# Loads of the convolution stage on one DMA queue, and a count of thresholds as the floor in the feed-forward block

## The chip, the cores and the metric

The kernel runs on all 8 cores of one Trainium2 chip, each on its own share of the sequence. The metric is the device time in microseconds of the slowest core. Each core has a matrix engine (TensorE, PE in the profile), a vector engine (VectorE, DVE), an activation engine (ScalarE, ACT), GpSimd (POOL) and SyncE (SP). In this kernel POOL and SP compute nothing: they issue DMA transfers, each from a program of its own that runs strictly in order.

## The reference

For x of shape 2 x 4096 x 2048, one layer of two branches that start from the same normalized input:

```python
xn = layernorm(x)
# branch 1: gated long convolution
q, k, v = xn @ Wq.T + bq, xn @ Wk.T + bk, xn @ Wv.T + bv     # 2048 x 2048 each
q, k = dwconv3(q), dwconv3(k)                                # along the sequence
kv = k * v
y = irfft(rfft(kv, n) * rfft(ssm_kernel, n), n)[..., :L]     # causal, 2048 taps
attn = ((y + kv * D_skip) * q) @ Wo.T + bo
# branch 2: feed-forward
h = xn @ W1.T                                                # 2048 -> 8192
a = gelu(clip(round(h / 0.1), -32768, 32767) * 0.1)
ffn = a @ W2.T
out = x + attn + ffn
```

## The kernel before

Each core owns 1024 rows of the output and gets a slab of 3328 rows, for the history of the convolution. The program is a row of stages with a full stop of all engines between them. `_phase1` normalizes the slab and prepares tables in bf16. `_phase2a` and `_phase2b` make kv and q. `_phase3` is the convolution, `_phase4` the projection with Wo, and `_phase5` the feed-forward block with the final sum. The order within a stage is written out by hand: each engine's instructions are put in a list, with waits on counting semaphores (`Builder.wait`, `Builder.tok`, `Builder.dma`, whose `dma_start` is line 196). The last instruction of a step on TensorE raises `T`, each VectorE instruction `V`, each ScalarE instruction `A`. `tok` (line 205) also makes each VectorE instruction wait for the one before it.

**The convolution (`_phase3`, from line 710).** The 2048 channels are taken in `GR` = 4 groups of 512, and each group in four steps.

1. Forward transform: 34 jobs (17 blocks of 128 frequencies, real and imaginary part), each of 24 matmuls (line 807). VectorE copies each result into `X` (line 823, tiles `p_xr` and `p_xi`). Each job needs a table `tf` of 1 MB, loaded by POOL into one of two buffers. Behind each of these loads POOL issues a load `wc` of a piece of W1 and SP a store of it as bf16 (`w_bf`), until 128 pieces are done.
2. If there is a next group, SP issues 32 DMA transposes that bring its kv into the other `kvg` buffer.
3. Pointwise product: for each of the 17 blocks SP loads the real and the imaginary part of the kernel's transform, `p_kr` and `p_ki` (`Kh`, 128 KB each, two buffers). Before block kc it waits until VectorE is done with block kc-2 (lines 840 to 844). VectorE then does six bf16 operations on 128x512 (lines 851 to 861) in place on `X`.
4. Inverse transform: after the last block, TensorE takes 34 tables `ti` (`p_ti`, 256 KB each, four buffers), each with 8 matmuls (line 881). The tables are loaded by POOL and SP in turn (line 871), each after TensorE is done with the table four back. VectorE then forms `y2tm` (lines 895 to 902).

The lists of POOL and SP simply follow these steps, so what is queued ahead of a load on its engine decides when it is issued.

**The feed-forward block (`_phase5`, from line 979).** First W1: 64 blocks of 128 features by 2 halves of 512 rows, so 128 tiles, each of 16 matmuls (line 1039) into one of two PSUM banks. VectorE turns the tile into rounded and clipped values by seven operations on 128x512 in float32. They all use one set of buffers `ub, iib, fb, cb, mb, zb` (tiles `p_u`, `p_ii`, `p_f`, `p_c`, `p_m`, `p_z`), and ScalarE applies gelu (line 1072) from `zb`. The first operation (line 1053) reads PSUM; it waits for the tile's matmuls and for the gelu of the tile before, and TensorE's tile two later waits for it. The operation at line 1053 forms u = 10 h + 4096.5; the next two convert it to int32 and back; lines 1060 and 1062 take 1 off where the conversion went above u, so that the result is the floor. Then W2: 4 column blocks by 64 feature blocks of 8 matmuls (line 1095), whose weights POOL loads from float32 (`p_w<-w2T`), and the final sum.

Of the kernel before, what the change touches and what calls it, by code (L numbers as in the profile page):

```python
# [10 lines left out]
OP = mybir.AluOpType  # L11
# [698 lines left out]
def _phase3(nc, bld, g, env):  # L710
    rec = Rec()
# [5 lines left out]
    gKV = [bld.dsem(f"p3gKV{i}", "sync") for i in range(2)]  # L717
    TFD = 2
    gTF = [bld.dsem(f"p3gTF{i}", "gpsimd") for i in range(TFD)]
    gKH = [bld.dsem(f"p3gKH{i}", "sync") for i in range(2)]  # L720
    TID = 4
    gTI = [bld.dsem(f"p3gTI{i}", ("gpsimd", "sync")[i % 2]) for i in range(TID)]
    gWC = [bld.dsem(f"p3gWC{i}", "gpsimd") for i in range(2)]
    xWC = [bld.dsem(f"p3xWC{i}", "sync") for i in range(2)]
    gDR = bld.dsem("p3gDR", "gpsimd")
# [1 line left out]
    with ExitStack() as P:  # L727
# [52 lines left out]
        for gg in range(GR):  # L780
# [10 lines left out]
            for kc in range(KC):  # L791
                for ri in range(2):
                    gjob = gg * 2 * KC + job
                    par = gjob % TFD
                    eng = "gpsimd"
# [41 lines left out]
            pw_done = {}  # L837
            for kc in range(KC):
                kp = kc % 2
                if kc >= 2:  # L840
                    bld.wait(rec, "sync", "V", pw_done[kc - 2])
                elif gg >= 1:
                    last_same = KC - 1 - ((KC - 1 - kc) % 2)
                    bld.wait(rec, "sync", "V", pw_prev[last_same])
                for ri in range(2):
                    bld.dma(rec, "sync", gKH[kp],
                            Kh[kp][ri][:, :], env["khat_sp"][ri, kc, gg])
                bld.wait(rec, "vector", gKH[kp], bld.c[gKH[kp]])
                s = slice(kc * GSZ, (kc + 1) * GSZ)
                bld.run(rec, "vector", lambda E, s=s, kp=kp:  # L850
                        E.tensor_mul(tmp[:, :], X[0][:, s], Kh[kp][0][:, :]))
                bld.run(rec, "vector", lambda E, s=s, kp=kp:
                        E.tensor_mul(tmp2[:, :], X[1][:, s], Kh[kp][1][:, :]))
                bld.run(rec, "vector", lambda E, s=s, kp=kp:
                        E.tensor_mul(tmp3[:, :], X[0][:, s], Kh[kp][1][:, :]))
                bld.run(rec, "vector", lambda E, s=s, kp=kp:
                        E.tensor_mul(tmp4[:, :], X[1][:, s], Kh[kp][0][:, :]))
                bld.run(rec, "vector", lambda E, s=s:
                        E.tensor_sub(Z[0][:, s], tmp[:, :], tmp2[:, :]))
                pw_tok = bld.tok(rec, "vector", "V", lambda E, s=s:  # L860
                                 E.tensor_add(Z[1][:, s], tmp3[:, :], tmp4[:, :]))  # L861
                pw_done[kc] = pw_tok
            pw_prev = pw_done
            bld.wait(rec, "tensor", "V", pw_tok)
            first = True
            for kc in range(KC):
                for ri in range(2):
                    idx = kc * 2 + ri
                    gidx = gg * 2 * KC + idx
                    par = gidx % TID  # L870
                    eng = ("gpsimd", "sync")[par % 2]
                    if gidx - TID >= 0:
                        bld.wait(rec, eng, "T", inv_mm[gidx - TID])
                    v = bld.dma(rec, eng, gTI[par], ti[par][:, :],
                                env["tbli_sp"][ri, kc * 128:(kc + 1) * 128, :])
                    bld.wait(rec, "tensor", gTI[par], v)
                    last = (kc == KC - 1) and (ri == 1)

                    def pinvmm(E, tc, par=par, ri=ri, kc=kc, first=first,
                               last=last):  # L880
                        return E.matmul(bank(tc)[:, :GSZ],  # L881
                                        ti[par][:, tc * 128:(tc + 1) * 128],
                                        Z[ri][:, kc * GSZ:(kc + 1) * GSZ],
                                        start=first, stop=last)
                    for tc in range(TCHO - 1):
                        bld.run(rec, "tensor", lambda E, tc=tc, f=pinvmm: f(E, tc))
                    inv_mm[gidx] = bld.tok(
                        rec, "tensor", "T", lambda E, f=pinvmm: f(E, TCHO - 1))
                    first = False
# [89 lines left out]
def _phase5(nc, bld, g, env):  # L979
    rec = Rec()  # L980
# [14 lines left out]
    with ExitStack() as P:  # L995
# [7 lines left out]
        ub = sb("p5_u", (128, TJ), F32)  # L1003
        iib = sb("p5_ii", (128, TJ), mybir.dt.int32)
        mb = sb("p5_m", (128, TJ), F32)
        fb = sb("p5_f", (128, TJ), F32)
        cb = sb("p5_c", (128, TJ), F32)
# [17 lines left out]
        for fc in range(FCH):  # L1025
            par = fc % 2
            if fc >= 2:
                bld.wait(rec, ("gpsimd", "sync")[par % 2], "T", w1_tok[fc - 2])
            v = bld.dma(rec, ("gpsimd", "sync")[par % 2], gW1[par],
                        w1c[par][:, :],  # L1030
                        env["w1_bf"][fc * 128:(fc + 1) * 128, :])
            bld.wait(rec, "tensor", gW1[par], v)
            for tj in range(NTJ):
                bnk = job % 2
                if job >= 2:
                    bld.wait(rec, "tensor", "V", ev_tok[job - 2])

                def p5mm(E, b, par, hc, tj):
                    return E.matmul(  # L1039
                        bank(b)[:, :TJ],  # L1040
                        w1c[par][:, hc * 128:(hc + 1) * 128],
                        xn[:, hc * NOWN + tj * TJ:hc * NOWN + (tj + 1) * TJ],
                        start=(hc == 0), stop=(hc == ECH - 1))
                for hc in range(ECH - 1):
                    bld.run(rec, "tensor", lambda E, b=bnk, par=par, hc=hc, tj=tj:
                            p5mm(E, b, par, hc, tj))
                mt = bld.tok(rec, "tensor", "T", lambda E, b=bnk, par=par, tj=tj:
                             p5mm(E, b, par, ECH - 1, tj))
                bld.wait(rec, "vector", "T", mt)
                if ga is not None:  # L1050
                    bld.wait(rec, "vector", "A", ga)
                ev_tok[job] = bld.tok(rec, "vector", "V", lambda E, b=bnk:
                        E.tensor_scalar(ub[:, :], bank(b)[:, :TJ], 10.0, 4096.5,  # L1053
                                        OP.mult, OP.add))
                bld.run(rec, "vector", lambda E:
                        E.tensor_copy(iib[:, :], ub[:, :]))  # L1056
                bld.run(rec, "vector", lambda E:
                        E.tensor_copy(fb[:, :], iib[:, :]))  # L1058
                bld.run(rec, "vector", lambda E:
                        E.tensor_tensor(cb[:, :], fb[:, :], ub[:, :], OP.is_gt))  # L1060
                bld.run(rec, "vector", lambda E:
                        E.tensor_sub(mb[:, :], fb[:, :], cb[:, :]))  # L1062
                bld.run(rec, "vector", lambda E:
                        E.tensor_scalar(cb[:, :], mb[:, :], 4096.0, -32768.0,  # L1064
                                        OP.subtract, OP.max))
                qv = bld.tok(rec, "vector", "V", lambda E:
                             E.tensor_scalar(zb[:, :], cb[:, :], 32767.0, 0.1,  # L1067
                                             OP.min, OP.mult))
                bld.wait(rec, "scalar", "V", qv)
                ga = bld.tok(rec, "scalar", "A",  # L1070
                             lambda E, fc=fc, tj=tj:
                             E.activation(a[:, fc * NOWN + tj * TJ:  # L1072
                                            fc * NOWN + (tj + 1) * TJ],
                                          zb[:, :], AF.Gelu_apprx_tanh))
                job += 1
            w1_tok[fc] = bld.c["T"]
        bld.wait(rec, "tensor", "A", bld.c["A"])
        ev2, w2_tok, st2 = {}, {}, {}
        for eo in range(EON):
            for fc in range(FCH):  # L1080
                par = fc % 2
# [18 lines left out]
                for tc in range(TCHO - 1):  # L1100
                    bld.run(rec, "tensor", lambda E, tc=tc, f=w2mm: f(E, tc))
                w2_tok[(eo, fc)] = bld.tok(rec, "tensor", "T",
                                           lambda E, f=w2mm: f(E, TCHO - 1))
            mmt = bld.c["T"]
            for tc in range(TCHO):
                par = tc % 2
# [15 lines left out]
                elif eo >= 1:  # L1122
# [7 lines left out]
                    lambda E, par=par, eo=eo:  # L1130
# [23 lines left out]
```

How the kernel before makes its waits and increments, by code:

```python
        def fn(E, out=out, in_=in_, h=h, tr=transpose, slow=slow):  # L195
            E.dma_start(out=out, in_=in_, transpose=tr,
                        allow_slow_non_contiguous=slow).then_inc(h, 16)
# [3 lines left out]
    def wait(self, rec, eng, sem, v):  # L201
        h = self.sems[sem]
        rec.add(eng, lambda E, h=h, v=v: E.wait_ge(h, v))
# [1 line left out]
    def tok(self, rec, eng, sem, mk):  # L205
        prev = self.c[sem]
        self.c[sem] += 1
        v = self.c[sem]
        h = self.sems[sem]
        if prev:
            rec.add(eng, lambda E, h=h, prev=prev: E.wait_ge(h, prev))
        rec.add(eng, lambda E, mk=mk, h=h: mk(E).then_inc(h, 1))
        return v
```

## Time and profile before

| what | us |
|---|---|
| two runs | 5645.95 and 5849.39 |
| their median | 5747.67 |
| the profiled execution, its time | 5644.92 |
| its span, first to last instruction, core 0 | 5643.4 |
| spans of the other seven cores | 5569.3 to 5620.4 |
| TensorE busy (matmuls) | 3500.1 (62%) |
| VectorE busy | 1402.5 (25%) |
| ScalarE busy | 413.6 (7%) |

The profile is of core 0, the slowest. The shares of busy time are means over stages with different limits, so each stage has to be read by itself: by its stretch of time, its waits, and its instructions in order.

### The profile page before, as it was taken

The page shows a single profiled execution, that of the slowest core. Times are in us where ns is not written, and L with a number is a line of the kernel's source. Part 1 is how long each engine was busy: PE and PEld are TensorE (multiplying, and loading weights), DVE is VectorE, ACT ScalarE, POOL GpSimd, SP SyncE. Part 2 cuts the span into 40 slices and gives each one's busy share as a digit, 9 for nine tenths or more (in the row PEclk, how much of TensorE's full clock was granted, in tenths as well). Part 3 has the DMA queues.
Part 4 walks back from the last instruction along what each step waited for, and adds up shares of the span by engine and source line. Part 5 has one row for each costly group of instructions (what it writes and reads, how often), then busy time and mean ns, then how long its engine had stood idle before and what let it go on. Part 6 is the DMA issues. An engine that isn't in the chain of part 4 may idle for free. (4 is left out here: it accounts for less than half of the span.)

```text
span 5643.4 us, 52539 instructions; the slowest of 8 cores (5569.3 to 5643.4 us)
## 1 busy us (share of the span) xinstructions
PE 3500.1 (62%) x18560; PEld 1801.3 (32%) x18560; DVE 1402.5 (25%) x2784; ACT 413.6 (7%) x791; POOL 543.3 (10%) x1008
## 2 busy tenths in 40 slices
PE   3777741999990828378277278506666666464644
PEld 1333311888880413133133133202222222121211
DVE  0111130344441400210311311300377772101011
ACT  0111100222220100000000000001111110000000
POOL 0000010111111001011011011000000001111111
PEclk9889875999995969789689699857899999898988
DMA  9878779111106148558559468341311112333343
GB/s 180 189 180 203 186 207 145 31 31 39 39 24 87 25 117 221 145 150 218 140 152 231 126 167 228 106 79 32 83 49 49 49 49 38 64 46 68 42 70 69
DMA packets 419134, 614.48 MB, mean 109 GB/s; under 512 B 228928, under 2 KB 300608, under 8 KB 389312
## 3 DMA queue, kind: packets, MB, share of 16 engines
q0 software_dynamic: 120352, 384.98, 32.2%
q1 hardware_dynamic: 298528, 226.15, 13.7%
q8 instruction: 156, 2.56, 0.2%
q14 instruction: 98, 0.80, 0.0%
HBM read 578.90 MB, written 138.94 MB: 127 GB/s over the span
## 5 line engine op out<-in xcount | busy, mean ns | idle before, releaser
L807 PE MATMUL ps<-p_kvg,p_tf 128*128 128x512 bf16 x3264 | 766.7, 395 | 336.1 <-DMA p_tf<-tblf_sp 161.9
L1095 PE MATMUL ps<-p_w,p_a 128*128 128x512 bf16 x2048 | 519.4, 402 | 397.7 <-DMA p_w<-w2T 279.0
L360 PE MATMUL ps<-p_ssm,p_tf 128*128 128x512 bf16 x2176 | 541.4, 414 | 241.2 <-ACT p_kb L377 153.9
L1039 PE MATMUL ps<-p_xn,p_w 128*128 128x512 bf16 x2048 | 465.8, 381 | 246.9 <-DVE p_u L1053 216.3
L807 PEld LDWEIGHTS ps<-p_kvg,p_tf 128*128 128x128 bf16 x3264 | 322.5, 101 | 780.4 <-issue 446.6
L533 PE MATMUL ps<-p_xq,p_wk 128*128 128x256 bf16 x3328 | 367.4, 273 | 183.8 <-DMA p_ckb<-ckb 183.7
L1095 PEld LDWEIGHTS ps<-p_w,p_a 128*128 128x128 bf16 x2048 | 193.6, 102 | 723.5 <-issue 558.6
L360 PEld LDWEIGHTS ps<-p_ssm,p_tf 128*128 128x128 bf16 x2176 | 224.8, 105 | 557.2 <-issue 348.7
L533 PEld LDWEIGHTS ps<-p_xq,p_wk 128*128 128x128 bf16 x3328 | 326.4, 98 | 223.1 <-issue 184.5
L533 PE MATMUL ps<-p_xq,p_wv 128*128 128x256 bf16 x3328 | 365.4, 273 | 0.0
L1039 PEld LDWEIGHTS ps<-p_xn,p_w 128*128 128x128 bf16 x2048 | 192.1, 98 | 520.7 <-issue 310.3
L881 PE MATMUL ps<-p_xr,p_ti 128*128 128x512 bf16 x544 | 135.2, 393 | 341.5 <-DVE p_xi L861 341.5
L533 PEld LDWEIGHTS ps<-p_xq,p_wv 128*128 128x128 bf16 x3328 | 325.6, 98 | 37.7
L953 PE MATMUL ps<-p_wo,p_y2fm 128*128 128x512 bf16 x512 | 112.5, 383 | 202.4 <-DMA p_y2fm<-y2tm 202.4
L1125 DVE TENSOR_TENSOR p_t<-ps,p_xr 128x512 f32<-128x512 f32 x32 | 22.1, 691 | 865.6 <-PE ps L1095 802.5
L657 PE MATMUL ps<-p2b_xq,p2b_wq 128*128 128x512 bf16 (+1 forms) x768 | 120.7, 309 | 151.1 <-DMA p2b_xq<-xn_sp 142.1
L196 POOL DMA_DIRECT2D p_w<-w2T x256 | 135.5, 530 | 710.7 <-PE ps L1095 698.6
L1053 DVE TENSOR_SCALAR p_u<-ps 128x512 f32<-128x512 f32 x128 | 88.5, 692 | 456.4 <-PE ps L1039 333.8
L562 DVE TENSOR_SCALAR p_cvt<-p_kcm,p_ck,p_ckb 128x256 bf16<-128x256 bf16 x208 | 72.1, 347 | 483.2 <-ACT p_vcm L550 461.3
L418 DVE BATCH_NORM_STATS2 p_st<-p_x 128x6 f32<-128x512 f32 x104 | 72.2, 694 | 463.5 <-DMA p_x<-x_slab 454.7
L823 DVE CAST p_xr<-ps 128x512 bf16<-128x512 f32 x68 | 47.0, 691 | 559.8 <-PE ps L807 559.8
L881 PEld LDWEIGHTS ps<-p_xr,p_ti 128*128 128x128 bf16 x544 | 54.1, 100 | 410.7 <-issue 350.9
(78 smaller groups left out, 2217.1 us busy)
## 6 DMA issues: line engine op xcount, KB each, us to landing
p_tf<-tblf_sp POOLq DMA_DIRECT2D x136, 1024.0 KB, 7.3
tblf_sp<-p_tf SPq DMA_DIRECT2D x34, 1024.0 KB, 14.2
p_wc<-w_lay POOLq DMA_DIRECT2D x128, 256.0 KB, 7.1
w_bf<-p_wc SPq DMA_DIRECT2D x128, 256.0 KB, 5.8
p_w<-w2T POOLq DMA_DIRECT2D x256, 128.0 KB, 3.3
p_x<-x_slab POOLq DMA_DIRECT2D x26, 1024.0 KB, 10.7
p_tf<-fwd_cos POOLq DMA_DIRECT2D x17, 1024.0 KB, 12.7
p_tf<-fwd_sin POOLq DMA_DIRECT2D x17, 1024.0 KB, 10.2
```

Source lines behind the costliest of these rows:

```text
L196: E.dma_start(out=out, in_=in_, transpose=tr, allow_slow_non_contiguous=slow).then_inc(h, 16)
L360: return E.matmul(bank(b)[:, :GSZ], tf[par][:, sc * 128:(sc + 1) * 128], ssm_sb[:, sc * D + gg * GSZ:sc * D + gg * GSZ + GSZ], start=(sc = ...
L418: E.bn_stats(st6[:, 6 * i:6 * (i + 1)], xb[par][:, BCH * i:BCH * (i + 1)]))
L533: return E.matmul(bank(b)[:, :TT], w[:, hc * D + ec * 128:hc * D + ec * 128 + 128], xq[qpar][:, hc * XSP + qoff:hc * XSP + qoff + TT], sta ...
L562: E.tensor_scalar(cvt[:, :TT], kcm[par][:, base:base + TT], cks[:, ec:ec + 1], ckbs[:, ec:ec + 1], OP.mult, OP.add))
L657: return E.matmul(bank(b)[:, :w], wq[:, hc * D + ec * 128:hc * D + ec * 128 + 128], xq[:, hc * QWT + co:hc * QWT + co + w], start=(hc == 0 ...
L807: return E.matmul(bank(b)[:, :GSZ], tf[par][:, pc * 128:(pc + 1) * 128], kvg[kp3][:, pc * GSZ:(pc + 1) * GSZ], start=(pc == g.PC0), stop=( ...
L881: return E.matmul(bank(tc)[:, :GSZ], ti[par][:, tc * 128:(tc + 1) * 128], Z[ri][:, kc * GSZ:(kc + 1) * GSZ], start=first, stop=last)
L953: return E.matmul(bank(b)[:, :EOSZ], y2fm[:, hc * NOWN + tc * 128:hc * NOWN + tc * 128 + 128], wo[:, hc * D + eo * EOSZ:hc * D + (eo + 1) ...
L1039: return E.matmul(bank(b)[:, :TJ], w1c[par][:, hc * 128:(hc + 1) * 128], xn[:, hc * NOWN + tj * TJ:hc * NOWN + (tj + 1) * TJ], start=(hc = ...
L1053: E.tensor_scalar(ub[:, :], bank(b)[:, :TJ], 10.0, 4096.5, OP.mult, OP.add))
L1095: return E.matmul(bank(tc)[:, :EOSZ], a[:, fc * NOWN + tc * 128: fc * NOWN + tc * 128 + 128], w2c[par][:, :], start=(fc == 0), stop=(fc == ...
```

## The change

In `_phase3` the loads `Kh` and all loads `ti` are issued by POOL; before, `Kh` and every second `ti` were issued by SP. The waits that belong to them move along, and the order in which they stand among each other stays. In `_phase5` the floor is computed in another way: m = u - f, where f is the value converted to an integer and back, then a count of how many of the six levels -2, -1, 0, 1, 2, 3 are at or below m, added to f, and 4099 taken off instead of 4096. Since m is between -1 and 1, the count is 2 or 3 and the result is the same floor.

```diff
-    gKH = [bld.dsem(f"p3gKH{i}", "sync") for i in range(2)]
+    gKH = [bld.dsem(f"p3gKH{i}", "gpsimd") for i in range(2)]
     TID = 4
-    gTI = [bld.dsem(f"p3gTI{i}", ("gpsimd", "sync")[i % 2]) for i in range(TID)]
+    gTI = [bld.dsem(f"p3gTI{i}", "gpsimd") for i in range(TID)]
...
                 if kc >= 2:
-                    bld.wait(rec, "sync", "V", pw_done[kc - 2])
+                    bld.wait(rec, "gpsimd", "V", pw_done[kc - 2])
                 elif gg >= 1:
                     last_same = KC - 1 - ((KC - 1 - kc) % 2)
-                    bld.wait(rec, "sync", "V", pw_prev[last_same])
+                    bld.wait(rec, "gpsimd", "V", pw_prev[last_same])
                 for ri in range(2):
-                    bld.dma(rec, "sync", gKH[kp],
+                    bld.dma(rec, "gpsimd", gKH[kp],
                             Kh[kp][ri][:, :], env["khat_sp"][ri, kc, gg])
...
-                    eng = ("gpsimd", "sync")[par % 2]
+                    eng = "gpsimd"
...
                 bld.run(rec, "vector", lambda E:
-                        E.tensor_tensor(cb[:, :], fb[:, :], ub[:, :], OP.is_gt))
+                        E.tensor_sub(mb[:, :], ub[:, :], fb[:, :]))
                 bld.run(rec, "vector", lambda E:
-                        E.tensor_sub(mb[:, :], fb[:, :], cb[:, :]))
+                        E.tensor_single_scalar(cb[:, :], mb[:, :], -2.0,
+                                               OP.is_ge))
+                for lvl in (-1.0, 0.0, 1.0, 2.0, 3.0):
+                    bld.run(rec, "vector", lambda E, lvl=lvl:
+                            E.scalar_tensor_tensor(cb[:, :], mb[:, :], lvl,
+                                                   cb[:, :], OP.is_ge, OP.add))
                 bld.run(rec, "vector", lambda E:
-                        E.tensor_scalar(cb[:, :], mb[:, :], 4096.0, -32768.0,
+                        E.tensor_add(mb[:, :], fb[:, :], cb[:, :]))
+                bld.run(rec, "vector", lambda E:
+                        E.tensor_scalar(cb[:, :], mb[:, :], 4099.0, -32768.0,
                                         OP.subtract, OP.max))
```

How the instructions stand now at three places. SP at the end of the first group's forward transform, before: the loads of the kernel's transform (`p_kr`, `p_ki`) stand behind the 32 transposes of the next group's kv.

```order
L196 DMA w_bf<-p_wc 128x1024 [waits s_p3gWC0]
L196 DMA_TRANSPOSE p_kvg<-kv_sp 128x512 x32
L196 DMA p_kr<-khat_sp 128x512
L196 DMA p_ki<-khat_sp 128x512
L196 DMA p_kr<-khat_sp 128x512
L196 DMA p_ki<-khat_sp 128x512
L196 DMA p_kr<-khat_sp 128x512 [waits s_V]
```

Now SP goes from the transposes straight on to the stores of the next group's pieces of W1.

POOL at the same place, before: from the last table of the forward transform to its half of the inverse tables, then to the next group.

```order
L196 DMA p_tf<-tblf_sp 128x4096 [waits s_T]
L196 DMA p_wc<-w_lay 128x1024 [waits s_p3xWC0]
L196 DMA p_ti<-tbli_sp 128x1024 x2
L196 DMA p_ti<-tbli_sp 128x1024 [waits s_T] x15
L196 DMA p_tf<-tblf_sp 128x4096 [waits s_T]
```

POOL there after the change, with the 34 loads of the kernel's transform (the first seven of them and the last) ahead of all 34 inverse tables:

```order
L196 DMA p_tf<-tblf_sp 128x4096 [waits s_T]
L196 DMA p_wc<-w_lay 128x1024 [waits s_p3xWC0]
L196 DMA p_kr<-khat_sp 128x512
L196 DMA p_ki<-khat_sp 128x512
L196 DMA p_kr<-khat_sp 128x512
L196 DMA p_ki<-khat_sp 128x512
L196 DMA p_kr<-khat_sp 128x512 [waits s_V]
...
L196 DMA p_ki<-khat_sp 128x512
L196 DMA p_ti<-tbli_sp 128x1024 x4
L196 DMA p_ti<-tbli_sp 128x1024 [waits s_T] x30
L196 DMA p_tf<-tblf_sp 128x4096 [waits s_T]
```

So the `Kh` loads no longer have transposes ahead of them, and the first four inverse tables now stand behind the last `Kh` load.

VectorE in the W1 part, one tile before (s_T: the matmuls, s_A: the gelu of the tile before, s_V: VectorE's own last instruction):

```order
L1053 TENSOR_SCALAR p_u<-ps 128x512 [waits s_T,s_A,s_V]
L1056 CAST p_ii<-p_u 128x512 [waits s_V]
L1058 CAST p_f<-p_ii 128x512 [waits s_V]
L1060 TENSOR_TENSOR p_c<-p_f,p_u 128x512 [waits s_V]
L1062 TENSOR_TENSOR p_m<-p_f,p_c 128x512 [waits s_V]
L1064 TENSOR_SCALAR p_c<-p_m 128x512 [waits s_V]
L1067 TENSOR_SCALAR p_z<-p_c 128x512 [waits s_V]
```

And one tile after the change (the numbers of the lines shift):

```order
L1053 TENSOR_SCALAR p_u<-ps 128x512 [waits s_T,s_A,s_V]
L1056 CAST p_ii<-p_u 128x512 [waits s_V]
L1058 CAST p_f<-p_ii 128x512 [waits s_V]
L1060 TENSOR_TENSOR p_m<-p_u,p_f 128x512 [waits s_V]
L1062 TENSOR_SCALAR p_c<-p_m 128x512 [waits s_V]
L1066 SCALAR_TENSOR_TENSOR p_c<-p_m,p_c 128x512 [waits s_V] x5
L1069 TENSOR_TENSOR p_m<-p_f,p_c 128x512 [waits s_V]
L1071 TENSOR_SCALAR p_c<-p_m 128x512 [waits s_V]
L1074 TENSOR_SCALAR p_z<-p_c 128x512 [waits s_V]
```

Thirteen instructions stand where there were seven, in one chain.

## Rows read from the trace of the kernel before

**Rows 1.** Whole run, who waited for whom: us in total, times, longest.

```profile
PE ps L881 <- DVE p_xi L861: 341.5, 4, 95.9
PE ps L1039 <- DVE p_u L1053: 216.3, 124, 2.0
DVE p_tmp L851 <- DMA p_ki<-khat_sp: 120.4, 4, 40.9
```

**Rows 2.** Timeline, end of the first forward transform: start, us, engine, line, operation, [idle before].

```profile
2309.05 41.56 SPq L196 DMA_TRANSPOSE p_kvg<-kv_sp  x32
...
2314.04 0.69 DVE L823 CAST p_xi<-ps 128x512 bf16<-128x512 f32 x1 [8.50 <-PE ps L807]
...
2351.27 0.43 SPq L196 DMA_DIRECT2D p_ki<-khat_sp  x1
...
2353.56 0.42 DVE L851 TENSOR_TENSOR p_tmp<-p_xr,p_kr 128x512 bf16<-128x512 bf16 x1 [38.84 <-DMA p_ki<-khat_sp]
...
2356.74 0.42 DVE L851 TENSOR_TENSOR p_tmp<-p_xr,p_kr 128x512 bf16<-128x512 bf16 x1
```

**Rows 3.** Timeline, the first pointwise operation of the second, third and fourth group.

```profile
2772.38 0.43 DVE L851 TENSOR_TENSOR p_tmp<-p_xr,p_kr 128x512 bf16<-128x512 bf16 x1 [40.87 <-DMA p_ki<-khat_sp]
...
3185.06 0.42 DVE L851 TENSOR_TENSOR p_tmp<-p_xr,p_kr 128x512 bf16<-128x512 bf16 x1 [40.50 <-DMA p_ki<-khat_sp]
...
3546.73 0.42 DVE L851 TENSOR_TENSOR p_tmp<-p_xr,p_kr 128x512 bf16<-128x512 bf16 x1
```

**Rows 4.** Timeline, first group's inverse transform: TensorE's tables and a load by POOL.

```profile
2428.33 1.89 PE L881 MATMUL ps<-p_xr,p_ti 128*128 128x512 bf16 x8
...
2430.06 1.89 PE L881 MATMUL ps<-p_xi,p_ti 128*128 128x512 bf16 x8
2430.76 0.54 POOL L196 DMA_DIRECT2D p_ti<-tbli_sp  x1 [2.92 <-PE ps L881]
```

**Rows 5.** DMA issues, 2410 to 2470, then 2355 to 2405: count, KB, median us to landing.

```profile
p_ti<-tbli_sp POOLq DMA_DIRECT2D x15, 256.0 KB, 2.9
p_ti<-tbli_sp SPq DMA_DIRECT2D x15, 256.0 KB, 3.0
...
p_ki<-khat_sp SPq DMA_DIRECT2D x15, 128.0 KB, 2.2
```

**Rows 6.** DMA issues of the whole run, the pieces of W1.

```profile
p_wc<-w_lay POOLq DMA_DIRECT2D x128, 256.0 KB, 7.1
```

**Rows 7.** Stretches of core 0 (transposes, forward transform, W1): busy by engine, PEclk, DMA share, GB/s.

```profile
2309.00:2352.00 43.00, 4.86 (x17) 1.76 (x15) 0.69 (x1) 0.00 (x0) 0.00 (x0) 0.58 0.46 105
...
2493.00:2727.00 234.00, 187.61 (x795) 78.79 (x793) 22.81 (x33) 0.00 (x0) 35.04 (x66) 0.94 0.82 217
4003.00:4700.00 697.00, 465.84 (x2048) 192.08 (x2048) 484.21 (x896) 81.18 (x128) 17.75 (x33) 0.99 0.15 49
```

**Rows 8.** Timeline, one tile of the W1 part and the start of the next.

```profile
4400.60 0.69 DVE L1053 TENSOR_SCALAR p_u<-ps 128x512 f32<-128x512 f32 x1 [0.95 <-ACT p_a L1072]
...
4401.44 3.61 PE L1039 MATMUL ps<-p_xn,p_w 128*128 128x512 bf16 x16 [1.75 <-DVE p_u L1053]
...
4405.16 0.63 ACT L1072 ACTIVATE p_a<-p_z 128x512 bf16<-128x512 f32 x1 [4.73 <-DVE p_z L1067]
4405.97 0.69 DVE L1053 TENSOR_SCALAR p_u<-ps 128x512 f32<-128x512 f32 x1 [0.95 <-ACT p_a L1072]
```

**Rows 9.** Groups of VectorE instructions, whole run: busy us, mean ns | idle before.

```profile
L566 DVE SCALAR_TENSOR_TENSOR p_cvt<-p_kcm,p_ck,p_cvt 128x256 bf16<-128x256 bf16 x208 | 100.7, 484 | 22.4 <-DVE p_cvt L562 0.9
...
L1060 DVE TENSOR_TENSOR p_c<-p_f,p_u 128x512 f32<-128x512 f32 x128 | 88.6, 693 | 13.3
...
L1064 DVE TENSOR_SCALAR p_c<-p_m 128x512 f32<-128x512 f32 x128 | 54.6, 427 | 13.6
...
L689 DVE SCALAR_TENSOR_TENSOR p2b_cvt<-p2b_qpre,p2b_cq,p2b_cvt 128x512 f32<-128x512 bf16 x32 | 24.0, 751 | 3.3
```

## Prediction

> **What bounds the kernel now.** I read first the table of waits, for the two stages that the diff touches, then the timeline at the place of each wait, then the stretches by engine, and last the groups of instructions for durations.
>
> In the convolution TensorE stands still four times for the pointwise product, 341.5 us in all [rows 1]. It cannot start the inverse transform before VectorE has done all 17 blocks. VectorE itself waits for its first block's load: 120.4 us over four groups, 40.9 at most [rows 1]. The timeline tells why. VectorE is done with the forward transform at 2314.04 + 0.69 us, but SP is busy with 32 transposes from 2309.05 for 41.56 us, and issues the first block's `p_ki` only at 2351.27 [rows 2]. In the second and third group the same wait is 40.87 and 40.50 us. In the fourth, which has no next group to fetch, there is none [rows 3]. Nothing else is late there, so this wait is on the path.
>
> In the W1 part of the feed-forward block one tile takes 4405.97 - 4400.60 = 5.37 us [rows 8]. That is VectorE's chain and nothing else: 692 + 2 x 427 + 2 x 693 + 2 x 427 = 3786 ns of operations, 6 gaps of 13.3 / 128 = 0.104 us between them, and 0.95 us in which VectorE waits for the gelu of the tile that it has just finished [rows 8, 9]. The sum is 5.36 us. (The 692 is line 1053's 0.69 us; the two at 693 have the form of line 1060, the four at 427 that of line 1064.) TensorE does its 16 matmuls in 3.61 us, and before them waits 1.75 us for line 1053 [rows 8], 124 times and 216.3 us in all [rows 1]. So there VectorE has no slack, and each microsecond put on its chain is paid 128 times.
>
> **The change part by part.**
>
> *The queue of the `Kh` loads.* On POOL the first two blocks' loads stand right behind the last forward table, with no wait that is still open. They are issued while TensorE still works on the last jobs, and VectorE can go on 0.1 us after its last copy. What goes is 38.84 + 40.87 + 40.50 = 120.2 us [rows 2, 3].
>
> What is late next? A block takes VectorE 2356.74 - 2353.56 = 3.18 us [rows 2]. With two buffers, the loads for block kc are issued when block kc-2 is done, and hide if they take less than 3.18 us from there. On SP they do. On POOL two things are to be added. The reaction: in the inverse transform the matmuls that POOL waits for end at 2428.33 + 1.89 us, and it issues at 2430.76, 0.54 us later [rows 4]. And POOL spends 0.54 us on each issue [rows 4]. For landing the queues are equal, 2.9 against 3.0 us for the same 256 KB [rows 5], so I take 2.1 for `p_ki` where SP had 2.2. The first load's timeline (issued 2351.27, 2.2 us to land, used 2353.56) leaves 0.09 us for VectorE's start [rows 2, 5]. The sum is 0.54 + 0.54 + 2.1 + 0.09 = 3.27 us. With two buffers a block then takes the mean of 3.27 and 3.18, so 0.05 us more than now.
>
> For some 41.56 / 3.2 = 13 blocks of three groups the transposes now run beside the loads. They take 0.46 of the DMA engines [rows 7]. No row shows a load from POOL beside transposes. The lower bound is no slowing. The upper is a POOL load while the engines are 0.82 busy, as `p_wc` in the forward transform: 7.1 us to land [rows 6, 7], a delay of 0.54 + 0.54 + 7.1 + 0.09 = 8.27 us, and (8.27 + 3.18) / 2 = 5.72 us a block. A share of 0.46 is nearer to the free case. I take 0.5 us more to land, 0.25 us a block: 3 x 13 x 0.30 = 12 us, and 29 other blocks x 0.05 = 1 us. The term is -120 + 13 = -107 us.
>
> The Trainium skill has a rule that speaks against this part. "SBUF — State Buffer", section "Who interferes with whom", says that descriptors for a DMA issued from GpSimd are written by GpSimd itself, and that it is locked out while VectorE runs an operation in a two-port mode. By the same section `tensor_tensor` has no such mode, so the six operations of a block should leave POOL alone; by the trap as it is first told, the loads would starve, as in the second rival below. The trace has no POOL issue beside the six operations.
>
> *The queue of the `ti` loads.* All 34 are now POOL's, behind the last `Kh` load, which is issued 0.54 us after block 14 ends. Six issues of 0.54 us and 2.9 us to land make 0.54 + 3.24 + 2.9 = 6.7 us for the fourth table. TensorE starts when block 16 ends, 6.4 us after block 14, and comes to the fourth table three tables later. In the steady state a table lasts 1.73 us (2430.06 - 2428.33), four buffers leave 3 x 1.73 = 5.2 us, and a load needs 0.54 + 0.54 + 2.9 = 4.0 us at most [rows 4, 5]. So it costs nothing; the cover is 1.2 us, and if it were gone by 1 us, each load would pay a fourth of it, 34 x 4 x 0.25 = 34 us. POOL gets to the next group's `tf` one table later, 1.7 us, with the 17 us of `y2tm` work ahead. The transposes lose nothing: SP issues them when it did, and they have the pointwise product and the inverse transform to land in. The stores of W1 behind them no longer wait on SP for `ti`, but they wait for their own loads anyway. All this is 0.
>
> *The floor.* Per tile two `tensor_tensor` in float32 go (693 ns each) and two come. Added are one `tensor_single_scalar`, taken as the 427 ns of `TENSOR_SCALAR` in float32, and five `scalar_tensor_tensor`. Their nearest row is line 689: 751 ns for 128x512 with one bf16 and one float32 input. From 256 to 512 elements the form goes from 484 to 751 ns [rows 9], 1.04 ns an element and a fixed 217. Six more instructions bring six more gaps. The sum is 0.427 + 5 x 0.751 + 6 x 0.104 = 4.81 us a tile, and 128 x 4.81 = 615 us. Bounds: the row below is `tensor_tensor` at 693 (5 x 0.058 x 128 = 37 us less); the form at half its rate, since now both inputs are float32, is 217 + 2 x 534 = 1285 ns (342 us more); and 693 instead of 427 for the comparison is 34 us more. I take 751, as a float32 `tensor_tensor` with two such inputs shows nothing of a half rate (693 ns, with 534 for 512 elements by the slope above).
>
> The Trainium skill warns of that half rate: "Vector Engine (DVE) Microarchitecture Reference", section "Points that are easy to get wrong", says that the form with two SBUF sources that are not bf16 halves its throughput. No run so far shows it. By that rule the time is the first rival's; by line 689 it is the forecast.
>
> TensorE in this part: its 3.61 us of matmuls per 10.2 us of tile make it idle more, and in the stretch in which it stands almost idle its granted clock is 0.58, near the level of 1.2 GHz, instead of 0.99, that of 2.4 GHz [rows 7]. Even at 1.2 GHz a tile is twice 3.61, 7.2 us, under 10.2. So nothing hangs on the clock. The weight loads come every 20 us instead of every 10.7 and stay hidden. The W2 part is as before.
>
> **The sum.** 5644.9 (the profiled execution: 5643.4 of span and 1.5 around it) - 107 + 615 = 6153 us. The other run of before was 204 us slower, and the median shown, 5747.67, lies halfway; I forecast for executions like the profiled one.
>
> **The rivals.**
>
> *The half rate of the five new operations* (by the rule above): 6153 + 342 = 6495 us. For it: both inputs are float32 in SBUF, as in no row. Against it: `tensor_tensor` reads two such inputs at the full rate [rows 9].
>
> *The loads from POOL are the pointwise product's bound.* If they take 8.27 us throughout, all 15 blocks per group that have to wait cost 2.54 us: 4 x 15 x 2.54 = 152 us against the 13 counted, 6153 + 139 = 6292 us. For it: no margin is left (3.27 against 3.18), and VectorE and POOL work closely together there. Against it: the 2.9 us of POOL's `ti` loads.
>
> *The change does not bring the loads forward*: something else on POOL keeps them until SP's transposes are through. 6153 + 107 = 6260 us. Against it: the order shows nothing open ahead of them.
>
> *Not slower: the added operations lie beside other work.* If the W1 part were bound by TensorE, VectorE's chain could grow free, and only -107 would stay: 5538 us. This decides at 107 / 128 = 0.84 us a tile: what the six operations put on the path must be under 0.14 us each, and the cheapest row of such an operation is 0.427 + 0.104. It would need the wait of 1.75 us before each tile's matmuls to be due to something other than line 1053.
>
> **How the numbers follow.** The forecast gets 0.82, the half rate 0.07, loads from POOL as the bound 0.05, loads not brought forward 0.03, not slower 0.02 and what I don't see 0.01. The range reaches from 6080 (`tensor_tensor`'s 693 ns, no slowing by transposes, and 20 us for the spread among cores) to 6300, which takes in the two rivals on the loads and the 34 us for the comparison; the half rate stays outside. Faster by over 2% (about what a measurement of this kernel can tell from no change) 0.02, within it 0.01, slower 0.97.
>
> **What would show it.** Right: no wait of some 40 us at line 851; blocks of 3.2 to 3.5 us; three waits of TensorE for line 861 near 60 us instead of 95; a tile of the W1 part of 10.2 us, with 751 ns for each of the five operations and TensorE waiting some 6.5 us per tile for line 1053. Wrong: 1285 ns in those operations, blocks over 4 us with a wait for `p_ki` at each, or a tile clearly off 10.2 us.

## The result and the profile after

| | before | after |
|---|---|---|
| median of all runs, us | 5685.11 (10 runs) | 6134.93 (11 runs) |
| profiled execution, us | 5644.92 | 6131.05 |
| its span, slowest core, us | 5643.4 (core 0) | 6129.5 (core 4) |

The changed kernel is slower, by a ratio of 1.0837 with a 95% interval of 1.0794 to 1.0881. The forecast was 6153 us in a range of 6080 to 6300. (In some executions one die runs at a lower clock; the ratios leave these out.)

First the table of waits, whole run, of the changed kernel: who waited for whom, us in total, times, longest. It answers to [rows 1].

```profile
PE ps L1039 <- DVE p_u L1053: 489.8, 120, 5.3
...
PE ps L881 <- DVE p_xi L861: 257.7, 4, 67.7
...
DVE p_tmp L851 <- DMA p_ki<-khat_sp: 40.1, 40, 3.0
```

In the convolution TensorE waits 84 us less for the pointwise product. VectorE's waits for `p_ki` have changed in kind: before 120.4 us in 4 waits, now 40.1 us in 40. The three long waits, one in each group that has a next one, have gone, and short ones, at about every second block, have come.

The timeline of the changed kernel at the first group's pointwise product shows both; it answers to [rows 2].

```profile
2301.39 0.54 POOL L196 DMA_DIRECT2D p_kr<-khat_sp  x1
2301.92 0.54 POOL L196 DMA_DIRECT2D p_ki<-khat_sp  x1
...
2310.76 0.69 DVE L823 CAST p_xi<-ps 128x512 bf16<-128x512 f32 x1 [4.81 <-PE ps L807]
2311.56 0.43 DVE L851 TENSOR_TENSOR p_tmp<-p_xr,p_kr 128x512 bf16<-128x512 bf16 x1
...
2314.21 0.43 DVE L861 TENSOR_TENSOR p_xi<-p_tmp 128x512 bf16<-128x512 bf16 x1
2314.74 0.42 DVE L851 TENSOR_TENSOR p_tmp<-p_xr,p_kr 128x512 bf16<-128x512 bf16 x1
2315.17 0.54 POOL L196 DMA_DIRECT2D p_kr<-khat_sp  x1 [11.64 <-DVE p_tmp L851]
2315.26 0.42 DVE L853 TENSOR_TENSOR p_tmp<-p_xi,p_ki 128x512 bf16<-128x512 bf16 x1
2315.70 0.54 POOL L196 DMA_DIRECT2D p_ki<-khat_sp  x1
...
2319.07 0.43 DVE L851 TENSOR_TENSOR p_tmp<-p_xr,p_kr 128x512 bf16<-128x512 bf16 x1 [1.26 <-DMA p_ki<-khat_sp]
```

The first block's loads are out 9 us before VectorE needs them, and it goes on 0.11 us after its last copy. The third block's loads may be issued when line 861 of the first ends, at 2314.64. POOL reacts 0.53 us later, issues the two in 1.07 us, and the data are used at 2319.07, 4.43 us after the release. By then VectorE has been done with the second block for 1.26 us, since a block lasts 3.18.

DMA issues of the changed kernel, first in that stretch (2309 to 2352 us, beside the transposes), then in the fourth group's (3452 to 3505 us, without them): KB each, median us to landing.

```profile
p_ki<-khat_sp POOLq DMA_DIRECT2D x10, 128.0 KB, 3.1
...
p_ki<-khat_sp POOLq DMA_DIRECT2D x15, 128.0 KB, 2.4
```

So a `p_ki` load through POOL lands in 2.4 us when alone and in 3.1 beside the first group's transposes. Beside those of the second and the third group (2692 to 2731 and 3075 to 3114 us) it takes over a microsecond more:

```profile
p_ki<-khat_sp POOLq DMA_DIRECT2D x9, 128.0 KB, 4.2
...
p_ki<-khat_sp POOLq DMA_DIRECT2D x9, 128.0 KB, 4.3
```

In the W1 part, one tile of the changed kernel (timeline), against [rows 8]:

```profile
4404.70 0.69 DVE L1053 TENSOR_SCALAR p_u<-ps 128x512 f32<-128x512 f32 x1 [0.95 <-ACT p_a L1079]
...
4405.54 5.30 PE L1039 MATMUL ps<-p_xn,p_w 128*128 128x512 bf16 x16 [4.70 <-DVE p_u L1053]
...
4407.36 0.43 DVE L1062 TENSOR_SCALAR p_c<-p_m 128x512 f32<-128x512 f32 x1
...
4407.89 3.88 DVE L1066 SCALAR_TENSOR_TENSOR p_c<-p_m,p_c 128x512 f32<-128x512 f32 x5
4411.87 0.69 DVE L1069 TENSOR_TENSOR p_m<-p_f,p_c 128x512 f32<-128x512 f32 x1
...
4413.77 0.63 ACT L1079 ACTIVATE p_a<-p_z 128x512 bf16<-128x512 f32 x1 [9.25 <-DVE p_z L1074]
4414.58 0.69 DVE L1053 TENSOR_SCALAR p_u<-ps 128x512 f32<-128x512 f32 x1 [0.95 <-ACT p_a L1079]
```

A tile takes 4414.58 - 4404.70 = 9.88 us instead of 5.37. The five new operations last 3.88 us together, the gaps between them included. TensorE's wait has grown from 1.75 to 4.70 us and its matmuls from 3.61 to 5.30. The group of the new instructions, and then the stretches of the W1 and the W2 part (columns as in rows 9 and 7), say the same of the whole:

```profile
L1066 DVE SCALAR_TENSOR_TENSOR p_c<-p_m,p_c 128x512 f32<-128x512 f32 x640 | 443.0, 692 | 66.5
```

```profile
3928.00:5196.00 1268.00, 728.22 (x1994) 254.83 (x2033) 982.50 (x1664) 81.43 (x129) 17.77 (x33) 0.69 0.08 26
5196.00:6129.00 933.00, 523.80 (x2007) 195.87 (x2048) 66.43 (x96) 0.37 (x1) 169.10 (x318) 0.88 0.35 59
```

The new operations take 692 ns each. TensorE's granted clock in the W1 part is 0.69, where it was 0.99. Part of that belongs to this core: cores 4 and 5 had 0.70 over 3928 to 5170 us, the other six 0.73 or 0.74. On core 0, with 0.74, TensorE waits longer for line 1053, and the part is as long (first starts to last starts 3913.0 to 5170.4 us there, 3928.8 to 5186.7 on core 4):

```profile
3928.00:5170.00 1242.00, 706.64 (x1994) 247.22 (x1992) 963.41 (x1633) 79.02 (x126) 17.31 (x32) 0.74 0.08 26
```

```profile
PE ps L1039 <- DVE p_u L1053: 527.3, 125, 5.3
```

Where the time went, from the first and the last start of line 1053 (`p_u`) in both traces, first before (core 0), then after (core 4):

```profile
L1053 DVE TENSOR_SCALAR p_u<-ps x128: 690/692/692, 4013.0 to 4695.7; 128x512 f32<-128x512 f32 x128
```

```profile
L1053 DVE TENSOR_SCALAR p_u<-ps x128: 690/692/693, 3928.8 to 5186.7; 128x512 f32<-128x512 f32 x128
```

All that comes before the W1 part is 4013.0 - 3928.8 = 84 us shorter. The W1 part went from 682.7 to 1257.9 us, 575 more. The rest, up to the end of the span, went from 947.7 to 942.8, 5 less. The sum is +486, the difference of the two spans.

These are two different cores, so the small terms are worth less than they look. On all eight cores the W1 part took 682.6 to 682.9 us before and takes 1257.3 to 1258.1 now. What comes before it is 60 to 100 us shorter on the same core (medians of the cores 4001.1 and 3919.8, 81 less), and TensorE's waits for line 861 are 88 to 98 us shorter. The rest has medians of 922.0 and 922.6. That the 84 us are also what the waits of these two cores lost is a coincidence.

### The profile page after: what moved, and what is told of

Its sections match the earlier page's. It is cut to its first block and busy times, and to the rows that moved or that the text cites. A ratio compares the mean times of both kernels' runs of the same rounds, so it can differ in the third digit from the quotient of the medians.

```text
span 6129.5 us, 53837 instructions; the slowest of 8 cores (6069.5 to 6129.5 us)
## 1 busy us (share of the span) xinstructions
PE 3758.2 (61%) x18322; PEld 1866.9 (30%) x18560; DVE 1900.9 (31%) x3552; ACT 414.2 (7%) x791; POOL 653.9 (11%) x1212
## 5 line engine op out<-in xcount | busy, mean ns | idle before, releaser
L1039 PE MATMUL ps<-p_xn,p_w 128*128 128x512 bf16 x2007 | 733.9, 542 | 551.0 <-DVE p_u L1053 489.8
L1039 PEld LDWEIGHTS ps<-p_xn,p_w 128*128 128x128 bf16 x2048 | 256.8, 130 | 1028.1 <-issue 996.7
L1066 DVE SCALAR_TENSOR_TENSOR p_c<-p_m,p_c 128x512 f32<-128x512 f32 x640 | 443.0, 692 | 66.5
L881 PE MATMUL ps<-p_xr,p_ti 128*128 128x512 bf16 x533 | 133.6, 392 | 258.6 <-DVE p_xi L861 257.7
```

The costliest lines, as they stand in the source:

```text
L881: return E.matmul(bank(tc)[:, :GSZ], ti[par][:, tc * 128:(tc + 1) * 128], Z[ri][:, kc * GSZ:(kc + 1) * GSZ], start=first, stop=last)
L1039: return E.matmul(bank(b)[:, :TJ], w1c[par][:, hc * 128:(hc + 1) * 128], xn[:, hc * NOWN + tj * TJ:hc * NOWN + (tj + 1) * TJ], start=(hc = ...
L1066: E.scalar_tensor_tensor(cb[:, :], mb[:, :], lvl, cb[:, :], OP.is_ge, OP.add))
```

## The experiments

The change has two parts that do not meet. The theory was that they simply add up: less wait for the order of SP's list, more operations on VectorE's chain. Its rival was that one part hides or gives back some of the other. Where a ratio to the kernel before is given, its 95% interval stands with it; the other kernels are read by their profile alone. "Medians of the dies" are the medians of the spans of cores 0 to 3 and of cores 4 to 7.

**1. The loads alone.** The edit is the first half of the diff: `Kh` and `ti` on POOL, the floor as before.

> Only the change in the convolution: all Kh and ti loads on POOL, the floor as before. Theory (the two parts add up; the loads' part is worth the 84 us that TensorE's waits for line 861 lost in the profile after): 84 us less than before, ratio 0.985, the waits for line 861 some 258 us in all. Rival (part of the gain is given back in the next forward transform or in the feed-forward block, hidden in the whole change by the long W1 part): the same waits, but less than 40 us off the time. The prediction's own 107 us would be a ratio of 0.981.

Measured: ratio 0.979, interval 0.9711 to 0.9869. TensorE's waits for line 861 were 253.7 us, 88 less than before, and the medians of the dies were 91 and 87 us shorter (5517.9 against 5609.1, 5514.6 against 5601.9). Nothing was given back; the theory holds. The ratio's interval excludes the rival's 40 us, but does not tell 84 us from 107.

**2. The floor alone.** The edit is the second half of the diff, with the loads as before. It was run twice.

> Only the new floor, the loads as before. Theory: six more operations on VectorE's chain, five of 692 ns: 128 x 4.51 = 577 us more than before, ratio 1.102, a tile of 9.87 us. Rival (the lower granted clock of TensorE in this part also costs something, there or in the W2 part): more than 590 us, with a W2 part longer than before's 942 us.

> The floor-only kernel again, since the runs of the first time were mostly disturbed. Theory: 128 x 4.51 = 577 us more than before, ratio 1.102. Rival (a cost of TensorE's lower clock outside the W1 part): over 1.11 on cores of an undisturbed die.

Measured the first time: the profiled execution took 6273.53 us; there was no ratio. Its cores 0 to 3 took 6174.5 to 6208.7 us, while core 4 had a clock of 0.806 and a W2 part of 993 us. That looked like the rival. But the W2 part was long only on cores 4 and 5 (993 and 984 us), whose granted clock over 5279 to 6270 us was 0.77 and 0.79; on the other six, at 0.89 or 0.90, it took 898 to 938 us. The second time: ratio 1.1064, interval 1.1003 to 1.1125, the W1 part from 4019.9 to 5276.9 us, 574 more than before, and a W2 part of 5286.9 to 6203.9, 917 us. The ratio's interval reaches past the rival's 1.11. The medians of the dies do not: they were 571 and 587 us longer than before, ratios of 1.102 and 1.105, for the 577 us of the theory. So the rival falls: the W2 part need not be longer with the new floor, and the 993 us went with a lower clock that came in one execution and not in the other. The two halves add up: -0.021 and +0.106 are +0.085, and the whole is +0.084.

**3. What makes the blocks late: one more buffer.** On top of the first experiment:

```diff
-    gKH = [bld.dsem(f"p3gKH{i}", "gpsimd") for i in range(2)]
+    gKH = [bld.dsem(f"p3gKH{i}", "gpsimd") for i in range(3)]
...
-              for i in range(2)]
+              for i in range(3)]
...
-                kp = kc % 2
-                if kc >= 2:
-                    bld.wait(rec, "gpsimd", "V", pw_done[kc - 2])
+                kp = kc % 3
+                if kc >= 3:
+                    bld.wait(rec, "gpsimd", "V", pw_done[kc - 3])
```

(The wait for the group before counts by three in the same way.)

> The loads-only kernel with three buffers for Kh instead of two, so that a load is issued when block kc-3 is done and has 6.35 us. Theory (the blocks beside the transposes are late by the latency of one load through POOL, about 4.1 to 5 us against 3.18): VectorE's 40 us of waits for p_ki go to under 5 us, blocks last 3.18 us, and the time is some 36 us under the loads-only kernel. Rival (the transposes leave too little DMA bandwidth, or POOL's issuing is held up by VectorE): the waits stay above 20 us.

Measured: ratio 0.9769, interval 0.9697 to 0.9842. On the profiled core the waits for `p_ki` are gone altogether (up to 3.1 us are left on the others), and TensorE's are at 221.5 us:

```profile
PE ps L881 <- DVE p_xi L861: 221.5, 4, 55.8
```

That is some 55 us a group, for 17 blocks of 3.18 us. The transposes and VectorE still work beside the loads, and `p_ki` still takes 3.6 us to land beside the first group's, so neither the bandwidth nor POOL's issuing was short; only the time from release to use was too long for two buffers. The medians of the dies are 18 and 27 us under the first experiment, for 32 us of waits; by the ratio alone the two can't be told apart.

**4. Which share is POOL's: `Kh` on ScalarE's queue.** On the kernel before:

```diff
-                    bld.wait(rec, "sync", "V", pw_done[kc - 2])
+                    bld.wait(rec, "scalar", "V", pw_done[kc - 2])
...
-                    bld.dma(rec, "sync", gKH[kp],
+                    bld.dma(rec, "scalar", gKH[kp],
```

(The other wait and the semaphores move along.)

> The kernel before with the Kh loads alone on ScalarE's queue, which is idle there; ti as before. Theory (POOL's reaction of 0.54 us and its 0.54 us an issue make the loads late, and beside transposes landing takes longer on top): blocks of 3.2 to 3.6 us beside the transposes, waits for p_ki under 20 us, and some 100 to 115 us less than before. Rival (the transposes alone make the loads late, whatever the queue): waits for p_ki of 35 us or more, as in the profile after, and some 85 us less than before.

Measured: ratio 0.984, interval 0.9759 to 0.992, so 45 to 136 us less, which holds the numbers of both. TensorE waits 239.6 us for line 861, 102 less than before, and VectorE 20.4 us for `p_ki` (18.4 to 28.5 over the cores):

```profile
DVE p_tmp L851 <- DMA p_ki<-khat_sp: 20.4, 23, 2.1
```

The waits are near those of the theory, but the medians of the dies are 84 and 88 us under before, which is the rival's number and not 100 to 115. So ScalarE's queue shortens the waits, and that it is faster than POOL's (91 and 87 us) is not shown. Both theories had a share in the lateness. To tell them apart, here are the mean distances of line 851's starts in the second group, over the 12 blocks beside the transposes and over the last 4, each from the timeline:

| kernel | queue of `Kh` | first 12, us | last 4, us |
|---|---|---|---|
| before | SP, after the transposes | 3.17 | 3.17 |
| loads alone | POOL | 3.83 | 3.39 |
| `Kh` on ScalarE | ScalarE | 3.64 | 3.18 |
| three buffers | POOL | 3.17 | 3.17 |

The other two groups with transposes differ by some tenths: their first 12 blocks took 4.06 and 3.91 us with the loads alone, 3.76 and 3.64 through ScalarE.

Away from the transposes the blocks through ScalarE's queue are not late, and those through POOL are, by 0.2 us. Beside them the blocks through ScalarE are late too. The DMA issues of this kernel in the first group, beside the transposes, show why:

```profile
p_ki<-khat_sp ACTq DMA_DIRECT2D x9, 128.0 KB, 3.8
```

In its fourth group the same load takes 2.2 us. So the transposes lengthen the landing whatever the queue, and POOL adds its reaction and its issues.

**5. The order of SP's list alone.** On the kernel before: the block of transposes is moved behind the loop of the pointwise product, and all `ti` go to POOL so that none stands behind the transposes.

> The kernel before with Kh still on SP, but the transposes behind all Kh loads in SP's list (all ti on POOL, so that none stands behind the transposes). Theory (the 40 us waits were the order of SP's list and nothing else; and the blocks were late only beside transposes and through POOL): no wait for p_ki at all, blocks of 3.18 us, TensorE's four waits for line 861 some 221 us as with three buffers, and the forward transform of the next group not late. Rival (the transposes come too late for the next group, or collide with the inverse tables): the same short waits, but new waits of TensorE for p_kvg or p_ti that give back over 30 us.

Measured: 5534.9 us for the profiled execution, and medians of the dies 94 and 102 us under before. Of the waits for `p_ki` 2.6 us are left (1.7 to 8.8 over the cores), the waits of TensorE for the pointwise product are 223.7 us, and no wait for `p_kvg` came up besides the first group's.

```profile
DVE p_tmp L841 <- DMA p_ki<-khat_sp: 2.6, 5, 0.9
```

(Line 841 is the 851 of the others.) The inverse transform waits a little for its tables beside the transposes:

```profile
PE ps L881 <- DMA p_ti<-tbli_sp: 14.4, 15, 3.0
```

It was 5.7 us before. The theory holds in the main: the 40 us were the order of SP's list, and a queue of its own is not needed for that. The time gained is less than the 118 us of waits; 9 of the difference are these waits for `p_ti`, and the rest stays open.

**6. Constant or pointer.** On the floor-only kernel: three of the five levels come from a 128x1 tile.

```diff
-                for lvl in (-1.0, 0.0, 1.0, 2.0, 3.0):
+                for lvl in (-1.0, 0.0):
...
+                for li in range(3):
+                    bld.run(rec, "vector", lambda E, li=li:
+                            E.scalar_tensor_tensor(cb[:, :], mb[:, :],
+                                                   lv[:, li:li + 1],
+                                                   cb[:, :], OP.is_ge, OP.add))
```

> The floor-only kernel, with three of the five levels (1, 2, 3) read from a 128x1 tile instead of given as constants. Theory (the 751 ns of line 689 came from its scalar per partition, the 692 ns of the new operations from their constants): the three last 751 ns, the other two 692 ns, and the W1 part 128 x 3 x 0.059 = 23 us more than the floor-only kernel. Rival (751 came from the bf16 input): all five last 692 ns.

Measured, groups of VectorE instructions of this kernel:

```profile
L1074 DVE SCALAR_TENSOR_TENSOR p_c<-p_m,p_lv,p_c 128x512 f32<-128x512 f32 x384 | 288.6, 752 | 42.6
...
L1070 DVE SCALAR_TENSOR_TENSOR p_c<-p_m,p_c 128x512 f32<-128x512 f32 x256 | 177.3, 692 | 28.5
```

With everything else equal the scalar from a tile costs 60 ns. The W1 part went from 4017.1 to 5300.2 us, 26 us more than without it. So the row I had taken for the price, line 689, was dearer for its scalar and not for its input types.

**7. Three operations less.** On the floor-only kernel, levels -2, -1 and 0 only.

> The floor-only kernel with only the levels -2, -1 and 0: the floor is the same, since m never reaches 1. Theory (each operation on the chain is paid in full, 0.692 + 0.104 us): a tile of 9.87 - 3 x 0.796 = 7.48 us, 128 x 2.39 = 306 us less than the floor-only kernel. Rival (part of the chain lies beside the matmuls of a TensorE at the lower clock, 6.8 us a tile): less than 250 us off, with TensorE's waits for line 1053 near 0.

Measured: line 1053 starts from 4019.7 to 4973.0 us, so a tile of 953.3 / 127 = 7.51 us, and 304 us less than the floor-only kernel's W1 part. TensorE still waits 331.5 us for line 1053, so the rival falls. Each operation on the chain is paid in full.

**8. gelu off the chain.** On the floor-only kernel, two buffers for the input of gelu in turn, and line 1053 waits for the gelu of two tiles before.

> The floor-only kernel with two buffers for the input of gelu, so that line 1053 waits for the gelu of the tile before the last. Theory (the tile is VectorE's operations and gaps plus the 0.95 us of gelu): a tile of 9.87 - 0.95 + 0.10 = 9.02 us, 108 us less than the floor-only kernel, and VectorE without idle time above the gaps. Rival (TensorE or the loads set part of the tile): less than 60 us off.

Measured: line 1055 (that is the 1053 of the others) starts from 4041.0 to 5197.5 us, a tile of 9.11 us, and the part is 101 us shorter. VectorE's waits for ScalarE are gone; what is left above 9.02 are scattered gaps of 0.5 us in place of 0.1. The tile is the sum of VectorE's chain, this time with VectorE as its only member.

**9. A version that beats both.** `Kh` on POOL with three buffers, and a shorter floor: adding and taking off 1.5 x 2^23 in float32 rounds as the reference does.

```diff
-                        E.tensor_scalar(ub[:, :], bank(b)[:, :TJ], 10.0, 4096.5,
+                        E.tensor_scalar(ub[:, :], bank(b)[:, :TJ], 10.0, 12582912.0,
                                         OP.mult, OP.add))
...
+                        E.tensor_scalar(cb[:, :], ub[:, :], 12582912.0, -32768.0,
+                                        OP.subtract, OP.max))
```

(It takes the place of the conversions, the comparison and the two operations behind it.)

> Both findings used: Kh on POOL with three buffers, and the rounding by adding and taking off 1.5 x 2^23 in float32, which leaves three operations a tile (692 + 427 + 427 ns). Theory (the tile is VectorE's chain until that is shorter than TensorE's matmuls): chain 1.55 + 0.21 + 0.95 = 2.70 us, under TensorE's 16 matmuls of 3.45 us, so TensorE is the bound with about 3.5 us a tile: 128 x 1.87 = 239 us less in the W1 part, with the 120 us of the loads 5645 - 359 = 5286 us, ratio 0.936; no wait of TensorE for line 1053. Rival (TensorE keeps waiting for the bank or a weight load, now that a block of W1 is used up in 7 us): a tile over 4 us and a ratio above 0.95.

Measured: 5258.69 us median, ratio 0.9329, interval 0.9302 to 0.9355, against 0.936 expected; TensorE has no wait for line 1053. The waits and the stretch of the W1 part of this kernel:

```profile
DVE p_u L1053 <- PE ps L1039: 553.1, 127, 340.1
```

```profile
3879.00:4320.00 441.00, 436.18 (x1990) 198.53 (x2029) 197.87 (x384) 81.72 (x129) 17.52 (x33) 1.00 0.22 75
```

Line 1053 starts from 3879.0 to 4317.6 us, a tile of 3.45 us. The wait has turned round: now VectorE waits for TensorE (213 us in 126 waits; the longest, 340.1 us, lies before the first tile), and TensorE is busy 436 of 441 us at a clock of 1.00.

## Why the prediction was right

*The bound of the W1 part.* Right. The chain 4.81 us longer per tile was the main term, and it measured 575.2 / 127 = 4.53 us. The size was off by one duration, in the term 5 x 0.751: five operations at 751 ns were counted and took 692, 5 x 0.059 = 0.30 us a tile and 38 us in all. The lower bound named for them was the right value. I had chosen line 689 because it has the same operation; the sixth experiment shows that its extra 60 ns belong to its scalar from a tile. The forecast's bound from `tensor_tensor`, with the operands alike, was the better neighbour.

*The half rate*, the first rival, is refuted: 692 ns with both inputs in float32, the same as a `tensor_tensor`. It would have been 1285. The warning in the Trainium skill ("Vector Engine (DVE) Microarchitecture Reference", section "Points that are easy to get wrong") does not hold for this operation and shape.

*The wait behind the transposes.* Right: with three buffers TensorE's waits are 341.5 - 221.5 = 120 us shorter, as counted, and the experiment with SP's order (and `ti` on POOL) takes away 118 us without another queue for `Kh`.

*The lateness of loads through POOL.* The mechanism was right, the size too small: 13 us were counted, and VectorE's waits for `p_ki` were 40.1, of which 257.7 - 221.5 = 36 us were on the path. The reaction (0.53) and the issues (1.07 for two) came out as read. What was wrong are the two steps on landing. "I take 2.1 for `p_ki`" was 2.4 us alone, which makes the delay 3.57 us and the block 3.38; the fourth group's took 3.39. "I take 0.5 us more to land" beside the transposes, 2.6 in all, was 3.2, 4.2 and 4.3 us in the three groups (windows as above, the first over 2311 to 2350 us). By the forecast's own sum these make blocks of 3.78, 4.28 and 4.33 us, where it had 3.48, and the first 12 blocks of the three groups took 3.80, 4.13 and 4.17. So the loads' term was -84 between the two profiled cores (-81 by the medians before the W1 part) and not -107.

*POOL held up by VectorE* was not seen: each `p_kr` issue of the changed kernel took 537 to 544 ns, beside the six operations or not. That agrees with what the Trainium skill says of `tensor_tensor` in "SBUF — State Buffer", section "Who interferes with whom", that it has no two-port mode. (It also says that with both inputs in SBUF such an operation contends with GpSimd's reads; these issues show nothing of that.) In the W1 part POOL's loads do fall on operations that take 427 ns where those with two inputs take 692. There an issue is sometimes longer, as this one of the kernel before (timeline):

```profile
4016.83 0.72 POOL L196 DMA_DIRECT2D p_w<-w_bf  x1 [35.64 <-PE ps L1039]
4017.00 0.43 DVE L1067 TENSOR_SCALAR p_z<-p_c 128x512 f32<-128x512 f32 x1
```

It took 0.72 us instead of 0.53. In the changed kernel three of the 31 issues of that part, all beside line 1071, took 0.58, 0.58 and 0.69 us, and the others 0.53; on the other cores the longest took 0.76. Whether those operations run in such a mode no row says; if they do, it cost an issue 0.23 us at most in this part.

*The inverse tables.* Right: behind the last `Kh` load they cost nothing. In the profile of the changed kernel TensorE had no wait for `p_ti`, where before it had 5.7 us.

*TensorE's clock.* Right that nothing hangs on it. The granted clock fell to 0.69, between the levels of 1.2 and 2.4 GHz, the matmuls of the tile shown took 5.30 us instead of 3.61, and TensorE still waited 4.70. The wait was put at 6.5 us by the old 3.61; the sum of both is what the chain fixes. Cores 0 and 4 show it: 0.74 and 0.70 of clock, 527.3 and 489.8 us of waits, and 1257.4 and 1257.9 us for the part. With the chain shortened in the ninth experiment TensorE had no such pauses and had 1.00.

The two misses have opposite signs: the cost of the floor was put 40 us too high (615 for 575) and the gain of the loads 23 us too high (107 for 84). With the 5 us that the rest got shorter on these two cores the total was off by only 22 us, 6153 against 6131 for the profiled execution. That is closer than either term was, so the nearness of the total is luck; that both mechanisms were met is not.

## What to carry to other kernels

A stage whose period is one engine's chain of dependent operations pays for every added operation in full, its gap too, times the number of tiles; read the period from two starts of the same line, check that the chain adds up to it, and price a new operation by a row with the same kinds of operands, its scalar included. A DMA list is strictly in order, so a load that is needed first belongs ahead of a batch that is needed later; changing the order did as much here as another queue. With two buffers compare the time from release to use (reaction, issues, landing beside what then runs) with the period: where they are within some tenths of a microsecond, a third buffer takes nearly the whole wait away (here for 256 KB more of buffers).

## What was not expected of the hardware

- A `scalar_tensor_tensor` of 128x512 in float32 takes 692 ns with a constant and 752 ns with a scalar read from a 128x1 tile.
- POOL starts a load 0.53 us after what it waited for, and spends 0.54 us on an issue. In the fourth experiment ScalarE issued at 2322.26, 0.08 us after line 861 ended at 2321.76 + 0.42, in 0.33 us; the second load of the pair took 0.59 us to issue here and 0.45 to 0.46 in the fourth group, without transposes:

```profile
2321.76 0.42 DVE L861 TENSOR_TENSOR p_xi<-p_tmp 128x512 bf16<-128x512 bf16 x1
2322.26 0.33 ACTq L196 DMA_DIRECT2D p_kr<-khat_sp  x1
...
2322.61 0.59 ACTq L196 DMA_DIRECT2D p_ki<-khat_sp  x1
```

- 32 transposes that take 0.46 of the DMA engines lengthened the landing of `p_ki` a good deal, from 2.4 us to 3.2, 4.2 and 4.3 through POOL (changed kernel, three groups) and to 4.0, 3.3 and 3.5 (loads alone), and from 2.2 to 3.8, 3.6 and 3.4 through ScalarE's queue (each the median over some 36 to 39 us from the first pointwise operation on). The groups of one queue differ more than the queues do. The profile puts the transposes on queue q1, ScalarE's loads on q10 and POOL's on q0, so it is not one queue that they share; what in the transposes delays the loads stays open.
